# Queries rounded in rows and turned by transposing DMAs, in place of TensorE transposes

## The reference

```
q = layernorm(x);  k = v = ctx
ig, fg = [q,k,v] @ gate_w.T + gate_b            # two gates for each token and head
cs     = cumsum(log_sigmoid(fg))
log_D  = tril(cs[:,None] - cs[None,:]) + ig     # decay from token t to token s
D      = exp(log_D - rowmax(log_D))
C      = (q @ k.T / sqrt(32)) * D               # for each head
h      = (C / max(|sum C|, exp(-rowmax))) @ v
x1     = x + tanh(g0) * layernorm(h) * ln_scale
z      = square(relu(layernorm(x1) @ W_fc.T))   # 1024 wide
y      = z @ W_proj.T
out    = x1 + tanh(g1) * spikes(y) / 5          # spikes counts thresholds that y passes
```

## Time and profile before

| | us |
|---|---|
| median of 3 runs | 650.81 (650.64 to 652.63) |
| the profiled execution's own time | 652.49 |
| its span in the profile | 650.70 |
| PE busy | 586.0 (90%) |
| DVE busy | 540.4 (83%) |
| POOL busy | 485.6 (75%) |
| ACT busy | 483.0 (74%) |
| mean share of the 16 DMA engines by the main queue | 47.3% |
| mean granted clock of TensorE | 0.978 |

### The profile page before, as it was taken

How to read it: one execution, slowest core, us unless ns; L and a number is a source line. 1 busy time by engine, 2 the same in 40 slices (tenths; PEclk the granted TensorE clock), 3 DMA queues, 4 the chain that set the end, 5 groups by cost and what they waited for, 6 DMA issues and landing times.

```text
span 650.7 us, 17665 instructions
## 1 busy us (share of the span) xinstructions
PE 586.0 (90%) x6032; PEld 483.9 (74%) x6032; DVE 540.4 (83%) x1222; ACT 483.0 (74%) x1011; POOL 485.6 (75%) x531
## 2 busy tenths in 40 slices
PE   1266787799999999999999999999999999999995
PEld 0255677788787778888788878788778877787895
DVE  4878786878988899899989998899989898887444
ACT  4555676788777878888787888788887876777773
POOL 6257668887896969977997979787888788675642
PEclk9997798999999999999999999999999999999998
DMA  8915552745187154835476436916473507600101
GB/s 267 229 52 117 85 130 61 151 122 99 53 164 197 46 119 118 194 55 98 115 184 132 79 88 141 203 37 116 113 195 89 113 8 144 134 33 2 33 2 65
DMA packets 73192, 71.33 MB, mean 110 GB/s; under 512 B 8720, under 2 KB 68752, under 8 KB 73104
## 3 DMA queue, kind: packets, MB, share of 16 engines
q1 hardware_dynamic: 71888, 70.00, 47.3%
q10 hardware_dynamic: 1216, 0.21, 0.2%
HBM read 27.44 MB, written 8.39 MB: 55 GB/s over the span
## 4 chain that ended last, share of the span: by engine, by line
PE 61%; issue 10%; ACT 8%; DVE 7%; POOL 6%; DMA 0%; POOLq 0%; ACTq 0%; DVEq 0%
PE z_ps L1013 20%; PE y_ps L1077 18%; PE arg_ps L704 4%; PE qk_ps L719 3%; PE misc_ps L465 3%; PE misc_ps L531 2%; POOL sq_lo L1056 2%; POOL c_lo L748 2%; PE pv_ps L843 2%; PE pv_ps L766 2%; PE pv_ps L768 2%; ACT sq_hi L1035 2%; PE pv_ps L767 1%; POOL am_rest L639 1%; PE y_ps L1106 1%
## 5 line engine op out<-in xcount | busy, mean ns | idle before, releaser
L1056 POOL TENSOR_TENSOR sq_lo<-w_raw,sq_hi 128x512 fp32r<-128x512 f32 (+1 forms) x96 | 112.7, 1176 | 57.7 <-ACT w_raw L1036 56.8
L748 POOL TENSOR_TENSOR c_lo<-decay 128x512 bf16<-128x512 f32 x128 | 132.3, 1040 | 25.7 <-DVE decay L738 23.3
L1013 PE MATMUL z_ps<-x_hi,wfc_hi 128*128 128x512 f32 (+1 forms) x288 | 115.1, 400 | 3.8 <-ACT w_raw L1023 3.2
L1013 PE MATMUL z_ps<-x_hi,wfc_lo 128*128 128x512 f32 (+1 forms) x288 | 107.0, 372 | 0.0
L1013 PE MATMUL z_ps<-x_lo,wfc_hi 128*128 128x512 f32 (+1 forms) x288 | 106.9, 371 | 0.0
L738 DVE TENSOR_TENSOR decay<-qk_ps,decay 128x512 f32<-128x512 f32 x128 | 86.9, 679 | 23.3 <-PE qk_ps L719 17.1
L1077 PE MATMUL y_ps<-sq_hi,wpr_hi 128*128 128x512 f32 (+1 forms) x256 | 105.7, 413 | 0.4 <-POOL sq_lo L1056 0.4
L730 ACT ACTIVATE decay<-arg_ps,lqk_col 128x512 f32<-128x512 f32 x128 | 86.3, 675 | 19.4 <-PE arg_ps L707 18.6
L1077 PE MATMUL y_ps<-sq_lo,wpr_hi 128*128 128x512 f32 (+1 forms) x256 | 98.1, 383 | 0.0
L1077 PE MATMUL y_ps<-sq_hi,wpr_lo 128*128 128x512 f32 (+1 forms) x256 | 98.0, 383 | 0.0
L1056 POOL TENSOR_TENSOR sq_lo<-relu,sq_hi 128x512 fp32r<-128x512 f32 (+1 forms) x48 | 56.1, 1169 | 33.3 <-ACT relu L1036 33.2
(11 more groups left out here) (161 smaller groups left out, 1732.7 us busy)
## 6 DMA issues: line engine op xcount, KB each, us to landing
x_in<-x SPq DMA_DIRECT2D x32, 256.0 KB, 3.1
kT_in<-ctx_cols SPq DMA_DIRECT2D x32, 256.0 KB, 3.8
v_in<-ctx_rows SPq DMA_DIRECT2D x32, 256.0 KB, 3.2
k_stack<-kT_hi SPq DMA_DIRECT2D x64, 128.0 KB, 3.3
k_stack<-kT_lo SPq DMA_DIRECT2D x64, 128.0 KB, 3.6
q_stack<-qT_hi SPq DMA_DIRECT2D x64, 128.0 KB, 3.9
q_stack<-qT_lo SPq DMA_DIRECT2D x64, 128.0 KB, 4.1
out<-w_raw SPq DMA_DIRECT2D x32, 256.0 KB, 3.6
```

What stands on the lines that cost most here:

```text
L748: e.tensor_tensor(c_lo[i % NCH][:, :], c, top(c), ALU.subtract).then_inc(sem("c_lo"), 1)
L1013: ins = e.matmul(z_ps[:, tokens(q)], lhsT, rhs, start=(n == 0), stop=(n == len(terms) - 1))
L1056: e.tensor_tensor(sq_lo[n % NSQ][:, tokens(q)], relu[n % NRE][:, tokens(q)], sq_hi[n % NSQ][:, tokens(q)].bitcast(fp32), ALU.subtract).the ...
```

## The change

`q_T`, `q_hi` and `q_lo` go; in their place stand a `q_hi` and a `q_lo` that work on rows, SBUF to SBUF, and `turn_q`, which issues for each batch two transposing DMAs on SP's queue, one for each tile of 128 tokens. Each of them turns a tile 128x512 in bf16 (both parts, 256 channels each) into four blocks 128x128 of `qT`. The gate products and `stack_heads` wait for the DMAs' landing (`q_landed`) where they waited for the subtraction. The q entries leave the list of the bank's turns. `q_tok` (two buffers) is new, and `xln` is free again after `q_lo`. A reserve of SBUF that the program does not use is cut to make room.

```
-        qT_hi = [sb(f"qT_hi{i}", [P, DC, S], bf16) for i in range(NQ)]
-        qT_lo = [sb(f"qT_lo{i}", [P, DC, S], bf16) for i in range(NQ)]
+        q_tok = [sb(f"q_tok{i}", [P, ST, 2, D], bf16) for i in range(NXL)]
+        qT = [sb(f"qT{i}", [P, 2, DC, S], bf16) for i in range(NQ)]
+        qT_hi = [t[:, 0, :, :] for t in qT]
+        qT_lo = [t[:, 1, :, :] for t in qT]
...
-            order = [("q", 0), ("q", 1), ("g", 0), ("g", 1), ("gT", 0), ("gT", 1), ("fT", 0), ("q", 2), ("fT", 1),
+            order = [("g", 0), ("g", 1), ("gT", 0), ("gT", 1), ("fT", 0), ("fT", 1), ("g", 2), ("g", 3), ("gT", 2),
...
-                e.wait_ge(sem("q_T"), b - NXL + 1)
+                e.wait_ge(sem("q_lo"), b - NXL + 1)
...
-        def q_T(e, b):
-            e.wait_ge(sem("ident_ready"), 3)
-            e.wait_ge(sem("xln"), b + 1)
-            misc_turn(e, ("q", b))
-            transpose_rows(e, xln[b % NXL]).then_inc(sem("q_T"), 1)
+        def q_hi(e, b):
+            e.wait_ge(sem("xln"), b + 1)
+            if b - NXL >= 0:
+                e.wait_ge(sem(f"ld_q{b % NXL}"), 16 * ST * (b // NXL))
+            e.activation(q_tok[b % NXL][:, :, 0, :], xln[b % NXL][:, :, :], ACT.Copy).then_inc(sem("q_hi"), 1)
...
+        def q_lo(e, b):
+            e.wait_ge(sem("q_hi"), b + 1)
+            e.tensor_tensor(q_tok[b % NXL][:, :, 1, :], xln[b % NXL][:, :, :], q_tok[b % NXL][:, :, 0, :],
+                            ALU.subtract).then_inc(sem("q_lo"), 1)
...
-            e.activation(qT_hi[b % NQ][:, :, :], misc_chunks(), ACT.Copy).then_inc(sem("q_hi"), 1)
+        def turn_q(e, b):
+            e.wait_ge(sem("q_lo"), b + 1)
...
+            for t in range(ST):
+                dst = qT[b % NQ][:, :, :, t * P:(t + 1) * P].rearrange("p k c s -> p (k c) s")
+                e.dma_start(dst, q_tok[b % NXL][:, t, :, :].rearrange("p k d -> p (k d)"), transpose=True)\
+                 .then_inc(sem(f"ld_q{b % NXL}"), 16)
-            e.tensor_tensor(qT_lo[b % NQ][:, :, :], misc_chunks(), qT_hi[b % NQ][:, :, :],
-                            ALU.subtract).then_inc(sem("q_free"), 1)
+        def q_landed(e, b):
+            e.wait_ge(sem(f"ld_q{b % NXL}"), 16 * ST * (b // NXL + 1))
...
-            e.wait_ge(sem("q_free"), b + 1)
+            q_landed(e, b)
...
-    nc = bacc.Bacc("TRN2", target_bir_lowering=False, num_devices=1)
+    nc = bacc.Bacc("TRN2", target_bir_lowering=False, num_devices=1, dynamic_dma_scratch_size=4096)
```

More of the change, by code:

```diff
@@ L1187, in sync_program @@
+            turn_q(e, 8)
+            stack_heads(e, 6)
+            turn_q(e, 9)
+            for n in range(1, 4):
+                load_m_rows(e, 4 * n + 2)
+                load_a_rows(e, 4 * n + 2)
+                load_values(e, 4 * n + 3)
+                load_x(e, 4 * n + 7)
+                store(e, 2 * n - 2)
                 load_a_rows(e, 4 * n + 3)
                 load_m_rows(e, 4 * n + 3)
+                stack_heads(e, 4 * n + 3)
+                load_k(e, 4 * n + 6)
+                load_values(e, 4 * n + 4)
+                turn_q(e, 4 * n + 6)
@@ new lines, in sync_program @@
+            load_values(e, 20)
+            turn_q(e, 22)
+            load_x(e, 24)
+            load_k(e, 23)
+            store(e, 7)
+            turn_q(e, 23)
+            stack_heads(e, 20)
+            load_values(e, 21)
+            load_x(e, 25)
+            load_k(e, 24)
+            load_m_rows(e, 20)
+            load_a_rows(e, 20)
+            load_a_rows(e, 21)
+            load_k(e, 25)
+            load_m_rows(e, 21)
+            stack_heads(e, 21)
+            load_a_rows(e, 22)
@@ new lines, in sync_program @@
+            load_values(e, 22)
+            load_m_rows(e, 22)
+            load_x(e, 26)
+            turn_q(e, 24)
+            stack_heads(e, 22)
+            turn_q(e, 25)
+            load_values(e, 23)
+            load_x(e, 27)
+            store(e, 8)
+            load_a_rows(e, 23)
+            load_m_rows(e, 23)
+            stack_heads(e, 23)
+            load_k(e, 26)
+            load_values(e, 24)
+            turn_q(e, 26)
+            load_x(e, 28)
+            load_k(e, 27)
+            store(e, 9)
@@ L1663, in vector_program @@
             ln2_stats(e, 0)
+            q_lo(e, 5)
             cmul(e, 1, 1)
@@ new lines, in vector_program @@
+            out_step(e, 7)
+            h_norm(e, 17)
+            ln2_stats(e, 17)
+            cmul(e, 18, 2)
+            x1_step(e, 17)
+            q_lo(e, 23)
+            state_own(e, 18)
+            cmul(e, 18, 3)
+            ln3_stats(e, 17)
+            ln3_offset(e, 17)
+            ln1_stats(e, 24)
+            h_norm(e, 18)
+            cmul(e, 19, 0)
+            ln2_stats(e, 18)
+            gate_pre(e, 7)
+            gate_cumsum(e, 7)
+            gate_cummax(e, 7)
+            x2_lo_step(e, 17)
@@ new lines, in vector_program @@
+            ln2_stats(e, 19)
+            cmul(e, 20, 1)
+            cmul(e, 20, 2)
+            x1_step(e, 19)
+            q_lo(e, 24)
+            state_own(e, 20)
+            cmul(e, 20, 3)
+            ln3_stats(e, 19)
+            x2_lo_step(e, 18)
+            cmul(e, 21, 0)
+            ln3_offset(e, 19)
+            q_lo(e, 25)
+            h_norm(e, 20)
+            ln2_stats(e, 20)
+            cmul(e, 21, 1)
+            x1_step(e, 20)
+            cmul(e, 21, 2)
+            ln3_stats(e, 20)
@@ new lines, in vector_program @@
+            h_norm(e, 21)
+            cmul(e, 22, 3)
+            ln2_stats(e, 21)
+            x2_lo_step(e, 20)
+            x1_step(e, 21)
+            q_lo(e, 27)
+            state_own(e, 22)
+            ln3_stats(e, 21)
+            ln3_offset(e, 21)
+            ln1_stats(e, 28)
+            cmul(e, 23, 0)
+            h_norm(e, 22)
+            ln2_stats(e, 22)
+            gate_pre(e, 8)
+            gate_cumsum(e, 8)
+            x1_step(e, 22)
+            gate_cummax(e, 8)
+            x2_lo_step(e, 21)
```

1764 lines of the change are left out of this document (1163 added, 601 removed).

## The result

The changed kernel takes 732.43 us, the median of 4 runs (730.64 to 737.11), against 651.10 us for the kernel before in the same runs (650.64 to 652.63). The ratio is 1.1259, with a 95% interval of 1.122 to 1.1297: 12.6% slower, where 640 us and at most 656 were forecast. One of the four runs with four plain copies for each batch, further down, fell in the chip's slower state and is left out of its row; all other runs count.

The account below looks back on a forecast made before the run. PE's stream was taken to bound the loop: 650.7 - 10.3 (PE in the loop) - 2 (beginning) + 1.8 (grown idle) = 640.2, for a median run 640 us. The range was 629 to 656 us.

Parts of the forecast that it names:

- What bounds the kernel now: In the loop from 200 to 550 us PE's stream is the time, so an instruction taken off PE shortens the period.
- Rival B: In the loop, DVE's chains with ACT and PE take over as bound; half of 1.72 us a period lost, 647 us; chance 0.13.
- PE loses 32 groups: PE drops 32 groups of 4 transposes; 24 of them in the loop at 0.43 us each save 10.3 us.
- The sum: Whole span: 650.7 less 10.3 in the loop, less 2 in the beginning, plus 1.8 for grown idle, gives 640.2 us.
- SP gets 64 transposing DMAs: On SP's queue: each issue 0.63 us, at most 2.5; SP's waits have room, so a transfer costs its issue alone.
- DVE's subtraction: On DVE, reading SBUF instead of PSUM: 0.67 to 0.84 us against 0.68; 0 to 5 us extra, hidden under PE.
- The new latency: Rounding to gate products: 7.6 us must fit a lead of 9.4 to 11.6 us; a landing up to 7 is free.
- The 16 DMA engines: In the queue's engines each transfer costs about 0.56 us, at most 4.1; a period then uses 43.5 us, hidden.
- the break-even of 3.7: In a loop period, the DMA engines' time for each transfer, 3.7 us, from which the transfers would fill those engines.
- Rivals C: In each group's gate chain, the transfers land late, from 7 us; at a landing of 10.3 us, 666 us; chance 0.15.
- D: Transfers fill the queue's DMA engines, from 3.7 us each; at 4.1 us each the time is 657 us; chance 0.05.
- The bank's turns: In the beginning, 32 of 116 bank users go; 2 us gained, with 4 lost and 8 gained as the ends.

## Why the prediction was wrong

The 81 us in steps, each a difference of two runs: the rows' way and no transposes, no transfers, orders of before: 660.0 - 650.8 = +9; the changed orders: 720.5 - 660.0 = +60.5; the transfers: 732.4 - 720.5 = +12. The shares hang on the order of the steps. With the transfers put first into the orders of before (and the roundings moved ahead) it is 743.6 - 650.8 = +93, and the changed orders then take 11 away. Neither the transfers nor the orders are harmless: each alone costs over 60 us, and together they do not add up.

1. *"What bounds the kernel now"* failed in its conclusion that an instruction taken off PE shortens the period. The rows were right; full busy time in a period doesn't say how close the next ring is. The nearest engine's sum was 6 us below, but the rings' length isn't a sum of busy time. Rival B had this and gave it half of the 1.72 us a period; in the run with one of four transposes it was most of it.
2. *"PE loses 32 groups"*, the term of 10.3 us, is about right as PE's work (8.0 us less busy for three quarters of the transposes) and wrong as time: they were worth 2.5 us, and with all gone the orders of before gave no gain. Its remark that a transpose takes double in the beginning by the clock's lower level is not in the rows: the granted clock of that stretch is 1.00.
3. *"The sum" had no term for the changed orders.* It priced the lead of ACT's rounding and the bank's turns and took the rest of the re-ordering as free. With the transfers out this alone is 60.5 us, the largest failure, and none of the rivals had it: a change that re-orders five engines has the fit itself as a term.
4. *"SP gets 64 transposing DMAs"* was mis-sized twice. The issue is 1.25 us, inside the bounds of 0.63 to 2.5 but twice the value taken. And "it costs the issue alone", with room in SP's waits, is wrong: SP issues 45.3 us in a period of before, the 98.1 us of waits are real, and yet the same 80 us of SP cost 34 to 65 us of time in those orders, 12 in the changed ones. Long waits of a queue in order did not mean room for a transfer where something urgent stood behind it.
5. *"DVE's subtraction"* was inside its bounds in the changed kernel (820 ns, 680 from PSUM), and out of them in the run with the orders of before: 979 ns, 9.4 us more in all on DVE. A period of that run is 72.12 us, with DVE at 66.92, but a period of the kernel before can be 72.01; what the slower subtraction costs was not isolated.
6. *"The new latency"* held: the landing is 3.2 us, where up to 7 was free, and PE waited 2.5 us in all. *"The 16 DMA engines"* held in its conclusion only. A transfer takes 1.23 us of them and not 0.56; that is still far under the break-even of 3.7. The share of a period, 0.59 (0.62 forecast), comes near only because the period is longer: 0.59 x 83.14 = 49 us of them, against 43.5 forecast. Rivals C and D are out. Of the two rules weighed, that of Advanced Engine Details and Errata, X-Bar Transpose (TRN2), in the Trainium skill (as fast as regular transfers) agrees roughly for the landing, 3.2 us against 2.5 for plain copies in the same place, and neither for the issue nor for the engines' time (1.23 us against 0.54). The estimate of 5.2 us, four times the figure for one block in the Trainium skill's VectorE: DVE Perf Modes, The three transpose paths, is not borne out: four blocks landed in 3.2.
7. *"The bank's turns"* forecast 2 us gained in the beginning. The first exponents came 6.0 us later instead. Of that PE's wait for a transfer was 1.4 us; the rest came in behind it, where PE waits for DVE's `i_pre` and for the load of `m_rows`.

Open: which of the changed orders makes the loss in the changed kernel. No run gives it POOL's order of before and keeps the other four, or changes ACT's, DVE's or PE's alone, or has the changed orders with the transposes left on PE. No version beat the kernel before; the one that saves 2.5 us leaves work out.

## What to carry to other kernels

Before counting a saving on the busiest engine, ask what the second bound is; the cheapest test is to leave most of the instructions out and time it, before building their replacement. Price a moved operation by the queue it moves into: each microsecond of issue on an in-order queue cost 0.4 to 0.8 us in the orders of before, by what stood behind it, and 0.15 in the changed ones, though SP's waits in the kernel before sum to 268 of 651 us. And when all engines' orders are rewritten with a change, time the new orders without the change and the change without the orders: a sum of waits can match the loss and still not be its cause, and a wait that begins with the program is a loss only against the same start in the kernel before.

## What the hardware showed

A transposing DMA SBUF to SBUF takes 1.25 us of its issuing queue, for four 128x128 blocks of bf16 and for eight (1.28 us), where a plain one of the bytes of four blocks takes 0.57 to 0.60. The landing is 3.2 us for four blocks in the changed kernel (2.5 for plain copies there) and 2.6 to 4.3 in the other runs, 3.6 for eight in the run with one transfer a batch. It moves its 128 KB in 544 packets, all under 512 bytes, where a plain copy has 144, and it takes 1.23 us of the 16 DMA engines in the changed kernel, 1.38 with the constant tile in the kernel before, against 0.54 for a plain copy in both. The issue on ACT's queue took 1.33 us.
